# TensorE's expert jobs written out for eight row counts in place of three

## The reference, cut to what matters

```
logits  = xf @ Wr + br                      # xf: 1024 rows, layer-normed
thresh  = second largest logit of each row
weights = softmax(where(logits >= thresh, logits, -inf))
h       = gelu(einsum('td,edh->eth', xf, W1) + b1)      # 512 -> 2048, 8 experts
expert_out = einsum('eth,ehd->etd', h, W2) + b2         # 2048 -> 512
out     = sum over e of expert_out * weights
```

## Time and profile before

| | us |
|---|---|
| median of 3 runs | 1752.58 |
| lowest and highest | 1750.35, 1754.89 |
| the profiled execution: its own time | 1766.07 |
| its span, first to last instruction | 1764.2 |
| PE busy, of the span | 1677.1 |
| DVE, ACT, POOL busy | 880.1, 697.0, 306.3 |

### The profile page before, as it was taken

The page is one execution under the profiler, slowest core; times in us unless marked ns, Lnnn a source line. Parts: engine busy times, 40 slices in busy tenths (PEclk is TensorE's granted clock), DMA queues, the critical chain, the costliest instruction groups (busy, mean ns, idle before and its releaser), DMA issues.

```text
span 1764.2 us, 27021 instructions
## 1 busy us (share of the span) xinstructions
PE 1677.1 (95%) x10906; PEld 1410.4 (80%) x10906; DVE 880.1 (50%) x1592; ACT 697.0 (40%) x1314; POOL 306.3 (17%) x257
## 2 busy tenths in 40 slices
PE   7999999999999999999999978994999999999996
PEld 6888888888888888888888766773888888888985
DVE  4334443444444434444344566774768447548841
ACT  5333333333333333333333334443556345336631
POOL 3200211011101111011100341555211011001101
PEclk9999999999999999999999989995899999999998
DMA  6601820111101110111002630114656437427611
GB/s 223 221 5 52 134 68 20 39 55 55 50 8 52 55 52 7 52 55 52 7 7 91 221 112 28 57 41 140 233 140 209 138 94 230 145 88 237 219 34 21
DMA packets 54067, 165.10 MB, mean 94 GB/s; under 512 B 10581, under 2 KB 10965, under 8 KB 53377
## 3 DMA queue, kind: packets, MB, share of 16 engines
q1 hardware_dynamic: 38032, 131.88, 21.7%
q0 software_dynamic: 15888, 31.19, 8.5%
HBM read 143.54 MB, written 55.64 MB: 113 GB/s over the span
## 4 chain that ended last, share of the span: by engine, by line
PE 87%; ACT 3%; DVE 3%; DMA 3%; issue 2%; POOL 1%; another core or an unknown queue 0%; SPq 0%; ACTq 0%; POOLq 0%; DVEq 0%
PE psum L404 64%; PE psum L745 13%; PE psum L409 5%; PE psum L524 4%; ACT P L1331 2%; DMA out_x<-xg,meta 1%; PE psum L606 1%; DMA ya<-residuals 1%; POOL out_x L1567 0%; PE psum L678 0%; DMA xg<-expert_rows 0%; DMA raw<-in_Wv 0%; DMA xs<-in_x 0%; DVE mx L982 0%
## 5 line engine op out<-in xcount | busy, mean ns | idle before, releaser
L404 PE MATMUL psum<-ctx,Wk 128*128 128x512 f32 x1536 | 384.9, 399 | 0.0
L404 PE MATMUL psum<-Wv,ctx 128*128 128x512 f32 x1536 | 368.7, 389 | 0.0
L404 PEld LDWEIGHTS psum<-Wv,ctx 128*128 128x128 f32 x1536 | 288.3, 188 | 59.9
L404 PEld LDWEIGHTS psum<-ctx,Wk 128*128 128x128 f32 x1536 | 279.2, 188 | 55.6
L881 DVE SCALAR_TENSOR_TENSOR kT<-psum,bkc,kT 128x512 fp32r<-128x512 f32 x128 | 96.0, 750 | 387.7 <-ACT kT L1245 387.7
L404 PE MATMUL psum<-xgT,Wh 128*128 128x256 f32 (+2 forms) x1536 | 268.8, 327 | 4.9 <-issue 4.8
L404 PEld LDWEIGHTS psum<-xgT,Wh 128*128 128x128 f32 x1536 | 239.2, 191 | 26.4 <-issue 7.2
L745 PE MATMUL psum<-Wh,hs 128*128 128x512 f32 x1056 | 258.8, 391 | 0.0
L745 PEld LDWEIGHTS psum<-Wh,hs 128*128 128x128 f32 x1056 | 194.6, 188 | 36.9
L1245 ACT ACTIVATE kT<-psum,bkc 128x512 fp32r<-128x512 f32 x128 | 88.3, 690 | 248.3 <-PE psum L404 248.2
L1410 ACT ACTIVATE gl<-psum,b1c 128x512 f32<-128x512 f32 x128 | 88.0, 688 | 225.6 <-PE psum L404 225.6
(11 more groups left out here) (146 smaller groups left out, 1780.7 us busy)
## 6 DMA issues: line engine op xcount, KB each, us to landing
raw<-in_W SPq DMA_DIRECT2D x128, 512.0 KB, 4.2
expert_rows<-in_spare_rows SPq DMA_DIRECT2D x16, 1042.0 KB, 8.0
raw<-in_ctxT SPq DMA_DIRECT2D x32, 512.0 KB
xg<-expert_rows POOLq DMA_DIRECT2D x32, 256.0 KB, 5.5
low_parts<-Olo POOLq DMA_DIRECT2D x32, 128.0 KB, 2.4
oT<-low_parts SPq DMA_DIRECT2D x8, 512.0 KB, 4.9
out_x<-x SPq DMA_DIRECT2D x12, 256.0 KB
xs<-in_x SPq DMA_DIRECT2D x4, 512.0 KB, 7.2
```

Source lines behind the costliest of these rows:

```text
L404: mm = pe.matmul(dst, l, r, start=n == 0, stop=n == len(pairs) - 1)
```

## The change: what it does

TensorE's job is written out for eight widths. `go_on` compares the next expert's count with 128, 224, 256, 288, 336, 384 and 448 in turn and takes the first body that holds it. `up` has `width` columns, and `down` has as many chunks as cover the width. For a width of 128 the last step of `down` has one chunk, and its last matmul would have to raise both `y_ready` and `y_psum`. TensorE raises `y_ready` by an instruction of its own after waiting for `y_psum`. GpSimd's three widths, ACT, DVE and SP stay as they are.

```diff
         NARROW, MIDDLE, WIDE = 256, 384, 512
+        WIDTHS = (128, 224, 256, 288, 336, 384, 448, 512)
...
                 if i == 0:
-                    pe.wait_ge(xgT_lo, CH * q + width // P)
+                    pe.wait_ge(xgT_lo, CH * q + -(-width // P))
...
-                for c in range(width // P):
+                for c in range(-(-width // P)):
                     for m, (x, y) in enumerate(((0, 0), (0, 1), (1, 0))):
                         mm = pe.matmul(bank[3 + c], hr[x][:, c * P:(c + 1) * P], Wh[i][y][:, 512:1024],
                                        start=i == 0 and m == 0, stop=i == NI - 1 and m == 2)
-                    if i == NI - 1 and c == 0:
+                    if i == NI - 1 and c == 0 and width > P:
                         mm.then_inc(y_ready, 1)
                 mm.then_inc(y_psum, 1)
+                if i == NI - 1 and width <= P:
+                    pe.wait_ge(y_psum, n + 1)
+                    pe.sem_inc(y_ready, 1)
...
-                    pe.br_cond(rows_of[q] <= NARROW, f"job{q}_{NARROW}", f"over_narrow_{place}")
-                    with nc.body(f"over_narrow_{place}", valid_engines=only):
-                        pe.br_cond(rows_of[q] <= MIDDLE, f"job{q}_{MIDDLE}", f"over_middle_{place}")
-                    with nc.body(f"over_middle_{place}", valid_engines=only):
+                    over = [f"over_{width}_{place}" for width in WIDTHS]
+                    pe.br_cond(rows_of[q] <= WIDTHS[0], f"job{q}_{WIDTHS[0]}", over[0])
+                    for n, width in enumerate(WIDTHS[1:-1]):
+                        with nc.body(over[n], valid_engines=only):
+                            pe.br_cond(rows_of[q] <= width, f"job{q}_{width}", over[n + 1])
+                    with nc.body(over[len(WIDTHS) - 2], valid_engines=only):
                         pe.br(f"job{q}_{WIDE}")
...
-                for width in (NARROW, MIDDLE, WIDE):
+                for width in WIDTHS:
```

## The result

The changed kernel takes 1744.74 us, the median of 17 runs (1737.34 to 1750.16), and the kernel before takes 1752.13 us on the same chip, also in 17 runs (1748.66 to 1759.80). The ratio is 0.9951 with a 95% interval from 0.9940 to 0.9963. So the change saves 7.4 us, where 18.0 were forecast. The sign was right and the size was less than half. The median is 0.7 us outside the stated range.

The account below looks back on a forecast made before the run. TensorE was taken to set the pace, with DVE next in the narrow jobs. Gains of 19.5 us less 1.55 for branches made 18.0 net, taking 1752.58 us to 1734.6, range 1728 to 1744.

Parts of the forecast that it names:

- The price by width: TensorE matmuls: 0.42 ns a column plus some 12 ns fixed, but 112 ns taken for both 224 and 128 columns.
- rivals 1: fp32r matmuls under 256 columns run slower per column on TensorE; 1785 us, slower than before; chance 0.12.
- 2 (119 ns): Weight load paces TensorE at 119 ns, so jobs 1, 3 and 5 gain nothing; 1737 us; chance 0.12.
- Jobs 4 and 7: `up` narrowed 512 to 448 and 384 to 336, all of it counting: 5.1 and 3.85 us gained.
- Rival 3: TensorE's clock falls in idle stretches of job 0 and before job 7, or branches cost more; 1737 to 1741 us; 0.10.
- Job 0: `up` narrowed 384 to 288, gain partly lost to late weights of step 15: 5.2 us gained, bounds 4 and 8.
- Jobs 1, 3, 5: `up` narrowed 256 to 224, half lost to waits for rows in 3 and 5: together 2.5 us gained, bounds 0 and 5.
- Job 6: Narrowed 256 to 128 with one chunk; DVE becomes the bound at 2.21 us a step: 2.9 us gained, bounds 0.5 and 4.
- Rival 4: Most gain swallowed: job 0 wholly, job 6 no shorter, narrow jobs nothing, clock and branches dear; 1748 us; chance 0.04.
- The branches: More comparisons and far branches between TensorE's jobs: together 1.55 us lost, bounds 1 and 3.
- the rest: Chance left over for the 128- and 288-wide jobs doing better, time below 1731 us.
- faster by more: Whole kernel faster by more than 0.3% (5.3 us): the forecast and rivals 2 and 3, chance 0.83.

Follow-up runs that it names:

- e7: The changed kernel, but at width 128 (job 6) `down` computes two chunks and no wait stands before the branch; 1739.60 us, ratio 0.9915 to the kernel before.
- c0: The kernel before, run and profiled once more with no edit; 1753.15 us, ratio 1.0004.
- e8: The changed kernel without width 128, with the next expert's rows transposed two steps later (9, 11, 13, 15); 1744.64 us, ratio 0.9851 to the kernel before.
- e2: The kernel before with only width 128 added to its widths 256, 384 and 512; 1787.64 us, ratio 1.0122 to the kernel before.
- e3: The changed kernel with a dummy matmul replacing TensorE's wait for `y_psum` before the branch at width 128; 1759.12 us, ratio 0.9953 to the kernel before.
- e10: The changed kernel with all eight widths and the next rows transposed two steps later; 1749.94 us, ratio 0.9890 to the kernel before.
- e1: The changed kernel without width 128, so job 6 runs at 224 columns; 1754.86 us, ratio 0.9927 to the kernel before.
- e5: The changed kernel without its widths under 256, so only jobs 0, 4 and 7 are narrower; 1735.98 us, ratio 0.9903 to the kernel before.
- e6: The changed kernel with only five widths (224, 288, 336, 448, 512), so fewer comparisons; 1739.51 us, ratio 0.9925 to the kernel before.
- e4: The changed kernel with ACT and DVE splitting the next expert's rows before the late weights; 1761.18 us, ratio 0.9968 to the kernel before.
- e11: The kernel before with only the next rows transposed two steps later, old widths kept; 1763.57 us, ratio 0.9968 to the kernel before.

## Why the prediction was right in sign and wrong in size

**The price by width: right.** Medians from start to start are 112 ns for 224 columns (taken: 112), 132 for 288 (133), 153 for 336 (155), 203 for 448 (200) and 112 for 128 (112). With this rivals 1 (143 ns and more) and 2 (119 ns) are out. The floor of 112 ns is the same at 128 and 224 columns (the means are 110 and 113), and at half clock both take 213. So it doesn't come from the moving columns, and the weight load is what is left. By the rule of the Trainium skill (TensorE: Matmul & The Clock Gate, section LDWEIGHTS (loading the stationary operand)), columns over 1.2, the load is estimated at 107 ns, and the trace is 5 above that in the median.

**Jobs 4 and 7: right, where the clock was full.** Job 4 gained 4.5 us (term 5.1, and 192 x 24 ns is 4.6). Job 7 takes 62.7 to 62.8 us in every kernel in which less than 1.3 us of idle time stood before it, a gain of 4.25 (term 3.85). In the change itself it gained only 2.2: 16 matmuls at 280 ns in place of 154 are 2.0 us. Rival 3 had this mechanism, with up to 3 us for it.

**Job 0: too small.** The term was 5.2 with bounds of 4 and 8, and 8.3 was measured. Over the profiles of the ten kernels with 288 columns (the change and nine experiments), job 0 takes 63.1 to 68.3 us, 64.5 in the mean: a gain of 3.3 to 8.5. What I took for the fixed lateness of one load isn't fixed. In the change there was next to no wait (PE busy 62.95 of 63.30 us), and that this execution had so little was luck: it covered 3.2 us of what was lost elsewhere. In e7, the slowest of the ten, TensorE stood 2.63 us for a gelu and had 3.4 us at half clock with it.

**Jobs 1, 3, 5: right in kind, a little optimistic.** I said that half of the gain in jobs 3 and 5 would turn into a longer wait for rows. The wait grew from 0.48 to 1.20 us (two executions of before, jobs 3 and 5) to 1.94 and 1.83, and in jobs 3 and 5 nothing of the gain was left, not half. The rows took only a part of it. The idle time at the branch behind these jobs grew as well, from 0.60 and 0.29 us (c0: 0.77 and 0.51) to 1.35 and 1.07. With job 1 and the branches they gained 0.1 us against a forecast of 1.35. In e8, with the rows turned later, both are smaller (no wait for rows, 0.55 us and nothing at the branches), and the gain is back. The forecast had also read the earlier trace rows too well: "all but 0.4 us" of idle time is 0.8 in job 6, and in jobs 3 and 5, which it didn't show, it was 1.6 and 0.8 already.

**Job 6: the step that failed.** It is this one: "So DVE becomes the bound. First cast 2.3 us after the job's start, 15 steps of 2.21, four splits of the next rows at 0.7, 1.1 for the last halves: 39.3 us; the last 3 matmuls end at 40.2." DVE did become the slower of the two, and its casts in the first part of the job are 2.21 us apart:

```profile
1606.23 0.43 DVE L1137 CAST hs<-gl 128x512 fp32r<-128x512 f32 x1 [1.24 <-ACT gl L1416]
1608.44 0.42 DVE L1137 CAST hs<-gl 128x512 fp32r<-128x512 f32 x1
```

TensorE's steps there are 2.04 us apart without a gap (1610.08, 1612.12, 1614.16), so the three steps between `up` and `down` still covered the difference. But the last matmul ended 44.9 us after the start and not 40.2. The forecast ran DVE as if it always had work, and here it fails: the weights came late. ACT stood 3.27 and 2.15 us for them, where in job 6 before it never stood more than 0.5, and DVE and TensorE stood behind it. Slow loads by themselves are not new: in c0, the kernel before, one of job 1 took 7.9 us. What is new is that a faster job asks for its weights sooner. (That the fetch of the rows is what made the loads slow is argued, not shown: no run took it away.) A late weight load I had named ("if a late weight load stops DVE too"). What I had not drawn is the next link: TensorE was idle for 4.14 us, and from 1.5 us into it had half its clock for 13.7 us. There 33 `up` matmuls took 213 ns in place of 112 and 6 `down` 427 in place of 227, 4.5 us more of PE time. DVE then waited for TensorE in turn: at half clock a step of this job is TensorE's again, as e2 shows. The other end of the job went nearly as said: 5.23 us to job 7 against 4.7, the wait before the branch being worth 1.4 of it (e3). Rival 3 had the clock in two places (job 0 and before job 7) and not in this one, which is the dear one. What makes the clock fall inside job 6 isn't settled, since in e10 it fell ahead of the long stop; that it costs these 4.5 us is read from the rows.

By the runs, then, the term of job 6 is not +2.9 but -2.3 in the profile, and with it goes 1.65 in job 7: together they gained nothing (-0.1) where 6.75 was forecast. e1, e5, e7, and e8 against e10 all say the same: without the width 128, or with the second chunk given back, jobs 6 and 7 together are 4.4 to 6.2 us shorter. Rival 4 (1748 us) is near the measured time, and in jobs 3, 5, 6 and 7 it had the loss in the main right; its other part, that job 0's gain is swallowed, didn't come.

**The branches: right in kind, dearer in this profile.** More comparisons cost 0.12 to 0.13 us each. Job 1 with the branch behind it has 1.1 us of idle time where the earlier trace rows have 0.35: 0.8 more for the forecast's 0.65. Before jobs 1, 4 and 6 it is 0.3, 0.75 and 0.8 us more; the last has no comparison more and was forecast at nothing, but its taken branch took 4.40 us in place of 3.61. Together that is 2.6 us for 1.55, within the bounds. The taken branch before job 2 differs by 0.5 us between the two executions of the kernel before (3.39 and 3.86), so the two comparisons that e6 spares against e1, 0.25 us, couldn't show. And the near branch that became far is hidden after jobs 2 and 4: their windows have PE busy but for 0.05 us. TensorE's branches after, by line (ns lowest/median/highest, first and last start):

```profile
L777 PEldq COMPARE_BRANCH  x8: 65/80/4397, 1217.4 to 1649.1; - x8
...
L780 PEldq COMPARE_BRANCH  x22: 65/65/4786, 1217.5 to 1649.6; - x22
```

**The sum.** Job by job the profile gains 12.8 us: the forecast's 18.0, plus 3.2 in job 0, less 5.2 in job 6, 1.65 in job 7 and 1.25 in jobs 1, 3 and 5, and 0.3 in the wide ones. The medians gain 7.4. The other 5.4 us are not in this profile, since it is that of the fastest run. Other executions with these widths show where they can go: in job 3 of e1, e3, e4 and e7 the rows were 2.67 to 5.48 us late, and behind each the clock was halved for 3.4 to 6.8 us, so that the job took 51.2 to 54.6 us where this profile has 48.9. In this profile, 1.94 us late, the clock stayed (as it did in e6's job 5 behind 2.77 us). Over the six kernels with 224 columns and the old turning (the change, e1, e3, e4, e6, e7), jobs 0, 1, 3 and 5 are in the mean 1.7, 0.4, 2.2 and 0.5 us longer than in this profile. By this estimate 4.8 of the 5.4 us lie there; no trace shows the median run itself.

The part before the experts, the same code in all, is not a matter of the change: the first `up` started at 1221.6 to 1224.9 us in the profiles of c0, e5, e6, e7 and the change, and at 1235.8 to 1240.6 in all others, the first profile of the kernel before and e11 among them. In the experiments it goes with the chip. The 13.5 us by which the profile before lay above its median are just this, 1238.4 - 1224.9. Against c0, whose time is near its median, the change's profile is 16.1 us shorter, 13.5 of it in the jobs.

Whether the forecast's other terms add up is best seen in e8, where the 128 and the late rows are out: against e11, the same kernel with the old widths on the same chip, it is 1763.57 - 1744.64 = 18.9 us faster. That this is near 18.0 is partly luck: 2.0 of it is job 6 at 224 columns, which the forecast didn't have, so 17 us stand against the 15.1 of its other terms. In the chances a small sum is off: the five that are named make 1.00 and leave nothing for "the rest", and the three taken for "faster by more" make 0.84, not 0.83.

## What to carry to other kernels

A gain on the engine that sets the pace counts until the next thing is late, so price a narrower step by what comes after it: the second engine with its real waits, the weights that are now asked for sooner, the rows that come when they come. On TensorE a new idle stretch costs more than its length, since the matmuls behind it may run at half clock; a job made lighter can take longer than the heavier one (128 columns 50.1 us, 224 columns 45.95). Where a wait for data lies in the path, first move the instruction that waits: here one line was worth 0.3% alone, and with it the widths of e1 gave 1.2% (e8 over e11) where they gave 0.7% without.

## What the runs showed of the hardware that was not expected

- A matmul with 128 x 128 fp32r weights has a floor of 112 ns in the median (mostly 107 to 115) from start to start, at 128 as at 224 moving columns; 256 columns take 119. At half clock 128 and 224 columns both take 213 ns, 288 take 240, 336 take 280 and 512 take 427.
- The clock can stay at half under work without a gap: in e2, 36.78 of 36.8 us busy with steps of twelve matmuls of 128 columns and three of 512, all at 1.2 GHz. In e7, with six of 512 a step and only 0.46 us idle ahead of it, the clock was full throughout job 6; which of the two differences did it, no run separates.
- Half-clock stretches in the middle of jobs of 224 and more columns lasted 3.4 or 6.8 us; inside job 6 at 128 columns they lasted 10.2 (e3), 13.7 (the change and e10) and 37.6 us (e2). The idle stretch with them was 1.68 us in e6 and 0.81 in e10, while 1.94 us in the change and 2.77 in e6's job 5 left the clock full, so its length alone doesn't decide.
- A taken branch to a far body took 3.3 to 5.9 us in these runs (5.86 before job 7 of e4), up to 1.8 us more than in the earlier trace rows.
- A load of one step's weights took 8.74 us from issue to landing in job 6, while the next rows were fetched too; the median of the 17 loads around it is 4.0 us.
